# Expert inputs gathered by a token list per slot instead of scattered row by row, with routing and experts in one block

## The reference, cut to what matters

```python
logits = xt @ router_w
probs = jax.nn.softmax(logits, axis=-1)
top1 = jnp.argmax(probs, axis=-1)
...
top2 = jnp.argmax(logits_no1, axis=-1)
...
loc1 = jnp.cumsum(m1, axis=0) - 1.0
loc2 = jnp.cumsum(m2, axis=0) - 1.0 + m1.sum(axis=0, keepdims=True)
C = 2 * math.ceil(T / E)
m1 = m1 * (loc1 < C)
m2 = m2 * (loc2 < C)
...
xin = jnp.einsum('tec,td->ecd', dispatch, xt)
h = jnp.einsum('ecd,edf->ecf', xin, fc1_w) + fc1_b[:, None, :]
h = jax.nn.gelu(h, approximate=False)
eout = jnp.einsum('ecf,efd->ecd', h, fc2_w) + fc2_b[:, None, :]
...
moe_out = jnp.einsum('tec,ecd->td', combine, eout).reshape(b, s, D)
return resid + moe_out
```

## Time and profile before

| what | value |
|---|---|
| median of three runs | 2062.14 us |
| the three runs | 2052.34, 2062.14 and 2062.99 us |
| the profiled execution | 2056.92 us |
| its span in the profile | 2055.2 us |
| busy: PE, DVE, ACT, POOL | 1669.1, 1533.7, 1170.0, 847.3 us |

### The profile page before, as it was taken

The page is one execution under the profiler, slowest core; times in us unless marked ns, Lnnn a source line. Parts: engine busy times, 40 slices in busy tenths (PEclk is TensorE's granted clock), DMA queues, the critical chain, the costliest instruction groups (busy, mean ns, idle before and its releaser), DMA issues. The chain is left out here.

```text
span 2055.2 us, 42001 instructions
## 1 busy us (share of the span) xinstructions
PE 1669.1 (81%) x15556; PEld 804.9 (39%) x15556; DVE 1533.7 (75%) x2709; ACT 1170.0 (57%) x2150; POOL 847.3 (41%) x1066
## 2 busy tenths in 40 slices
PE   5799999997799999999999627799999995501992
PEld 2666666664133333333332224233333332400771
DVE  4767888877899999999999367788888883550124
ACT  3232222225499898898988614577777774300332
POOL 1100000005488878778788525122121122074454
PEclk8789999998699999999999857799999998555996
DMA  2186000004101011001110035111111114111444
GB/s 80 63 139 88 0 0 0 0 0 144 32 21 37 20 22 37 20 22 31 26 21 5 23 87 150 38 38 34 36 32 38 39 23 98 48 48 51 138 134 143
DMA packets 96025, 103.06 MB, mean 50 GB/s; under 512 B 28288, under 2 KB 62800, under 8 KB 95344
## 3 DMA queue, kind: packets, MB, share of 16 engines
q1 hardware_dynamic: 91760, 92.33, 19.2%
q0 software_dynamic: 4096, 8.43, 1.2%
HBM read 63.65 MB, written 36.80 MB: 49 GB/s over the span
## 5 line engine op out<-in xcount | busy, mean ns | idle before, releaser
L1234 DVE TENSOR_REDUCE ba_at_top<-ps 128x2 f32<-128x1024 f32 x512 | 588.4, 1217 | 18.0 <-PE ps L1149 16.2
L1267 ACT ACTIVATE ba_at_ring<-ps 128x512 f32<-128x512 f32 x1024 | 556.9, 597 | 64.8 <-PE ps L1175 51.4
L1313 POOL TENSOR_TENSOR ba_at_ring<-ba_at_ring,rb_near 128x256 f32<-128x256 f32 (+2 forms) x640 | 483.2, 783 | 148.2 <-ACT ba_at_ring L1267 142.3
L1234 DVE TENSOR_REDUCE ca_at_top<-ps 128x2 f32<-128x1024 f32 (+3 forms) x384 | 348.6, 954 | 68.6 <-PE ps L1149 33.0
L1267 ACT ACTIVATE ca_at_ring<-ps 128x512 f32<-128x512 f32 (+1 forms) x640 | 318.7, 553 | 98.7 <-PE ps L1175 96.6
L1175 PE MATMUL ps<-qop,kop 49*128 49x512 bf16 (+3 forms) x1792 | 321.6, 367 | 35.2 <-DMA qop<-ca_at_negm 7.2
L1149 PE MATMUL ps<-kop,qop 48*128 48x512 bf16 (+3 forms) x1792 | 316.7, 368 | 32.2 <-DVE ba_at_top L1234 12.4
L1194 PE MATMUL ps<-ba_at_ring,ba_at_low 128*32 128x256 f32 (+1 forms) x4864 | 329.6, 358 | 12.7 <-ACT ba_at_osb L1254 9.8
L1303 POOL TENSOR_SCALAR_AFFINE_SELECT ca_at_ring<-ca_at_ring 128x512 f32<-128x512 f32 x128 | 80.0, 637 | 359.3 <-ACT ca_at_ring L1267 359.2
L520 ACT ACTIVATE gm_sg<-ps,gm_bias 128x512 f32<-128x512 f32 x128 | 88.1, 688 | 235.0 <-PE ps L460 235.0
L1175 PEld LDWEIGHTS ps<-qop,kop 49*128 49x128 bf16 x1792 | 81.5, 93 | 351.2 <-ACT ba_at_ring L1267 189.0
(11 more groups left out here) (316 smaller groups left out, 1728.6 us busy)
## 6 DMA issues: line engine op xcount, KB each, us to landing
cs_fc<-in_fc_w SPq DMA_DIRECT2D x32, 256.0 KB, 2.7
qk_parts<-ba_at_ring SPq DMA_DIRECT2D x24, 256.0 KB, 3.7
qop<-qk_parts SPq DMA_DIRECT2D x64, 96.0 KB
kop<-qk_parts SPq DMA_DIRECT2D x64, 96.0 KB
qk_parts<-ca_at_ring SPq DMA_DIRECT2D x24, 256.0 KB, 3.6
ex_xi<-expert_rows_in SPq DMA_DIRECT2D x16, 258.0 KB, 3.1
expert_rows_in<-gm_zero SPq DMA_DIRECT2D x1, 4096.0 KB
expert_rows_out<-gm_zero SPq DMA_DIRECT2D x1, 4096.0 KB
```

The lines of the kernel that those rows point to most:

```text
L1234: nc.vector.tensor_reduce(top[:, k0 // CH, half, :, pair, i % HB], k.ps[:, slot:slot + 2, 0:k1 - k0], AX.X, ALU.max).then_inc(a_read, 1)
L1267: nc.scalar.activation(ring[:, ring_of(u, n) * HG + t % HG, 0:width(n)], k.ps[:, B_BANK + bank_of(u, t), 0:width(n)], ACT.Exp).then_inc(ex ...
L1313: ins = nc.gpsimd.tensor_tensor(w, w, a.near[:, u % NG * HG + j, lo - (i - 1) * P:hi - (i - 1) * P], ALU.mult)
```

## The change

The rows of the tokens are no longer sent to slots. SP writes the normalised tokens once, in token order, to `expert_rows_in` (four plain DMAs, now 4096 rows of 128 words). For each of the 8192 slots the kernel makes the number of the pair that sits in it, as a table `cs_rows` of 128 x 64 integers (slot = 128 times column plus partition), and POOL gathers the rows of an expert by four indirect DMAs that read, `ex_xi` from `expert_rows_in`. The same table, in its other half, tells where the results go.

The table is made with matmuls. For each choice DVE splits the slot number of each token into column and partition (a cast, a shift, an and, a cast back) and makes two one-hot arrays in bf16: `ids`, 128 x 32 x 64, which has a one at the slot's column, and `same`, 128 x 32 x 128, which has a one at its partition. They lie in the tiles `qop` and `kop` of the attention, which are free by then. ACT multiplies `ids` by the token's partition number, POOL by its tile number, and PE adds `same` transposed times these over the 32 tiles: 64 matmuls of 128 x 128 x 128 in all, into one bank. Seven small DVE instructions turn the sums into row numbers, with a row of its own for each unused slot.

`route` and `experts` become one block: `experts` now hands back five functions that each engine calls at the end of its part of `route`. `ex_xi` and `ex_eo` have four buffers instead of two, the loop over experts is written out, and POOL fetches three experts ahead. The addition of the gated hidden state to `x_tok` moves from the end of `route` into the loop over experts on DVE, a quarter after each of four experts. The zeroing of `expert_rows_in` in the first mixture, the copy of the tokens on ACT and the row-number column go away.

```diff
-                sp.dma_start(k.rows_in[0:E * CAP, 0:D].rearrange("(p a) d -> p a d", p=P),
-                             zero[:, 0:D].unsqueeze(1).broadcast_to([P, E * CAP // P, D])).then_inc(cleared, 16)
-                sp.dma_start(k.rows_in[0:E * CAP, D:D + 1].bitcast(I32).rearrange("(p a) b -> p (a b)", p=P), m["unused_rows"],
-                             allow_slow_non_contiguous=True).then_inc(cleared, 16)
...
+                for b in range(B):
+                    sp.wait_ge(dve_plain, (b + 1) * TB // 2)
+                    sp.wait_ge(act_plain, (b + 1) * TB // 2)
+                    sp.dma_start(k.rows_in[b * L:(b + 1) * L, :].rearrange("(t p) d -> p t d", p=P),
+                                 r.xt[:, b * TB:(b + 1) * TB, :]).then_inc(r.sent, 16)
+                then.sync(sp)
...
+                for i in range(2):
+                    pe.wait_ge(weighed, i + 1)
+                    pe.wait_ge(by_tile, i + 1)
+                    for t in range(NT):
+                        ins = nc.tensor.matmul(k.ps[:, 7, 0:2 * NSLOT], same[:, i, t, :],
+                                               ids[:, i, t, :, :].rearrange("p o c -> p (o c)"),
+                                               start=i == 0 and t == 0, stop=i == 1 and t == NT - 1)
+                ins.then_inc(tabled, 1)
+                then.tensor(pe)
...
-                for b in range(B):
-                    ts = slice(b * TB, (b + 1) * TB)
-                    nc.scalar.copy(r.xt[:, 1, ts, 0:D], r.xt[:, 0, ts, 0:D]).then_inc(copied, 1)
+                for i in range(2):
+                    act.wait_ge(alike, i + 1)
+                    nc.scalar.activation(ids[:, i, :, 1, :], ids[:, i, :, 0, :], ACT.Copy,
+                                         scale=rc[:, T_PART:T_PART + 1]).then_inc(weighed, 1)
...
-                send_copies(nc, k, r, 0)
-                pool.wait_ge(to_ready, 2)
-                pool.wait_ge(copied, B)
-                send_copies(nc, k, r, 1)
+                    pool.wait_ge(weighed, i + 1)
+                    tile = rc[:, T_TILE + i * NT:T_TILE + (i + 1) * NT].unsqueeze(2).broadcast_to([P, NT, NSLOT])
+                    nc.gpsimd.tensor_tensor(ids[:, i, :, 0, :], ids[:, i, :, 0, :], tile, ALU.mult).then_inc(by_tile, 1)
+                then.gpsimd(pool)
...
-                    vec.tensor_copy(r.to[:, i, :], row[:, i, :]).then_inc(to_ready, 1)
+                    L_(vec.tensor_copy(numi[:, 0, :], row[:, i, :]))
+                    L_(vec.tensor_scalar(numi[:, 1, :], numi[:, 0, :], 7, None, ALU.logical_shift_right))
+                    L_(vec.tensor_scalar(numi[:, 2, :], numi[:, 0, :], P - 1, None, ALU.bitwise_and))
+                    L_(vec.tensor_copy(numf[:], numi[:, 1:3, :]))
+                    vec.tensor_tensor(ids[:, i, :, 0, :], rc[:, T_IOTA:T_IOTA + NSLOT].unsqueeze(1).broadcast_to([P, NT, NSLOT]),
+                                      numf[:, 0, :].unsqueeze(2).broadcast_to([P, NT, NSLOT]), ALU.is_equal)
+                    vec.tensor_tensor(same[:, i, :, :], rc[:, T_IOTA:T_IOTA + P].unsqueeze(1).broadcast_to([P, NT, P]),
+                                      numf[:, 1, :].unsqueeze(2).broadcast_to([P, NT, P]), ALU.is_equal).then_inc(alike, 1)
...
+                dve.wait_ge(tabled, 1)
...
+                vec.tensor_scalar(r.rows[:, 1, :], r.rows[:, 0, :], TOK - 1, None, ALU.bitwise_and).then_inc(table_ready, 1)
+                then.vector(dve)
...
+    def gpsimd(pool):
+        def fetch(e):
...
+            if e >= XB:
+                pool.wait_ge(turned, e - XB + 1)
+            for q in range(QT):
+                at = e * QT + q
+                nc.gpsimd.indirect_dma_start(xi[:, e % XB, q, :], None, k.rows_in,
+                                             bass.IndirectOffsetOnAxis(ap=r.rows[:, 1, at:at + 1], axis=0)).then_inc(x_in[e % XB], 16)
...
+        def give(e):
+            pool.wait_ge(eo_ready, e + 1)
...
+        pool.wait_ge(r.table_ready, 1)
+        pool.wait_ge(r.sent, B * 16)
+        for e in range(XB - 1):
+            fetch(e)
+        for e in range(E):
+            if e + XB - 1 < E:
+                fetch(e + XB - 1)
+            give(e)
...
+        turn(0)
+        for e in range(E):
+            if e + 1 < E:
+                turn(e + 1)
+            upper(e)
+            if e:
+                lower(e - 1)
+        lower(E - 1)
```

More of the change, by code:

```diff
@@ L1572, in flat, with _ @@
             return t[:].rearrange("p t e -> p (t e)")
+        then = experts(nc, k, m, r, c)
         with nc.Block() as block:
-            block.sync(r.loads)
+            @block.sync
+            def _(sp):
+                r.loads(sp)
+                for b in range(B):
[4 more added lines that the diff above has]
+                then.sync(sp)
             @block.tensor
@@ new lines, in scalar @@
+    def scalar(act):
+        act.wait_ge(consts_in, 32)
+        for e in range(E):
+            for f in range(FB):
+                act.wait_ge(up, e * FB + f + 1)
+                if f == 0 and e >= 2:
+                    act.wait_ge(down, e - 1)
+                nc.scalar.activation(hh[:, e % 2, f, :], k.ps[:, 2 + f, :], ACT.Gelu, bias=b1[:, e, f:f + 1]).then_inc(act_done, 1)
+        act.wait_ge(r.g_ready, 1)
+        for t in range(NT):
+            n = t // 4
+            if t % 4 == 0:
+                act.wait_ge(got[n % 4], (n // 4 + 1) * 2 * 16)
+            y1 = back[:, 0, n % 4, t % 4, :]
+            nc.scalar.activation(y1, y1, ACT.Copy, scale=r.g[:, 0, t:t + 1]).then_inc(first, 1)
@@ new lines, in vector, with turned_in, out, residual @@
+    def vector(dve):
+        dve.wait_ge(consts_in, 32)
+        def turned_in(e):
+            dve.wait_ge(turned, e + 1)
+            if e >= 2:
+                dve.wait_ge(up, (e - 1) * FB)
+            nc.vector.tensor_scalar(xT[:, e % 2, :], k.ps[:, e % 2, :], r.ln2[:, 0:1], r.ln2[:, 1:2], ALU.mult, ALU.add).then_inc(xT_ready, 1)
+        def out(e):
+            dve.wait_ge(down, e + 1)
+            if e >= OB:
+                dve.wait_ge(eo_out[e % OB], QT * 16 * (e // OB))
+            row = b2[:, e:e + 1, :].broadcast_to([P, QT, D])
+            nc.vector.tensor_tensor(eo[:, e % OB, :, :], k.ps[:, 6 + e % 2, :].rearrange("p (q d) -> p q d", d=D), row, ALU.add).then_inc(eo_ready, 1)
+        def residual(b):
+            h = r.hidden[:, b * TB:(b + 1) * TB, :]
+            xs = k.x[:, b * TB:(b + 1) * TB, :]
+            nc.vector.tensor_tensor(h, h, k.row[:, 2, b:b + 1, :].broadcast_to([P, TB, D]), ALU.mult).then_inc(gated_h, 1)
+            dve.wait_ge(gated_h, b + 1)
+            nc.vector.tensor_tensor(xs, xs, h, ALU.add).then_inc(x_plain, 1)
+        def add(n):
+            xs = k.x[:, 4 * n:4 * n + 4, :]
+            dve.wait_ge(gated, n + 1)
+            dve.wait_ge(x_plain, B)
+            nc.vector.tensor_tensor(xs, xs, back[:, 1, n % 4, :, :], ALU.add).then_inc(summed, 1)
+        turned_in(0)
+        for e in range(E):
+            if e + 1 < E:
+                turned_in(e + 1)
+            if e:
+                out(e - 1)
+                if e % 3 == 0 and e // 3 <= B:
+                    residual(e // 3 - 1)
+        out(E - 1)
+        for t in range(NT):
+            dve.wait_ge(first, t + 1)
+            y1, y2 = back[:, 0, t // 4 % 4, t % 4, :], back[:, 1, t // 4 % 4, t % 4, :]
+            nc.vector.scalar_tensor_tensor(y2, y2, r.g[:, 1, t:t + 1], y1, ALU.mult, ALU.add).then_inc(both, 1)
+            if t % 4 == 3 and t >= 7:
+                add(t // 4 - 1)
+        add(NCH - 1)
@@ L2010, in causal_sublayer @@
         route(nc, k, m, r)
-        experts(nc, k, m, r)
 def program(nc, m):
```

329 lines of the change are left out of this document (112 added, 217 removed).

## The result

| | median | executions |
|---|---|---|
| before | 2058.93 us | 12 (2051.04 to 2063.84) |
| after | 2068.57 us | 12 (2060.73 to 2073.44) |

The ratio is 1.0049, with a 95% interval of 1.0036 to 1.0062: some 10 us slower, on the line between "no change" and "slower" that the prediction drew at 0.5%. The forecast was 2065.

The account below looks back on a forecast made before the run. POOL's issuing of 128 indirect DMAs behind the table was to bound the experts. At full clock -4.7 us, plus 10.7 for clock falls, made +6.0 on the profiled 2056.92, 2062.9, and 1.7 more gave 2065 us; range 2044 to 2086.

Parts of the forecast that it names:

- What bounds: Experts: POOL's issuing bounds, eight issues or 10.13 us an expert against PE's 7.45; 128 issues are 161.9 us.
- The table: Ahead of the experts: added DVE instructions +7.3 us; POOL's first fetch at 1841.7, 43.2 later than the old first send.
- A fetch's price: POOL's gathers: a fetch costs what a send costs, a pitch of 1.265 us; no indirect read in the trace before.
- rivals of a dearer and of a cheaper fetch: POOL's fetch pitch: 1.48, about 2078 us, chance 0.26; or 1.0 or less, about 2041 to 2046, chance 0.16.
- second rival: L1792 on POOL: fetch pitch 1.48, +19.8 us, about 2078; passes 0.5% from about 1.38 on; chance 0.26.
- fourth rival: POOL's issuing is hardly a cost, so PE bounds from about 1854: -41 us, about 2018; chance 0.04.
- The waits: POOL in the expert loop: start 5.7 us, middle none if PE's clock holds, end 6.5; residual pieces slow it 1.4.
- The clock: PE: 2.7 us pauses drop the clock every second expert, some six times, +10.7 us; earlier 1.6 us pause fell, 1.3 held.
- slack of 0.57: Middle experts: the chain from fetch end to dependent give, 9.56 us, stays under POOL's 10.13 us an expert.
- The rival in which the clock holds: PE during the experts: no clock falls, so -4.7 us, about 2054; chance 0.15.
- What was put at nothing: First mixture's zeroing, at most -2 us; SP's token writes, far ahead of 1841; SP's loads and ACT's copy, off the path.
- The sum: Whole kernel: -4.7 us at full clock, +10.7 for clock falls, together +6.0; forecast 2065 us.

Follow-up runs that it names:

- the run with two fills: Kernel after, four buffers, PE running two matmuls of constants before each turn from the fourth expert on: 2064.29 us, ratio 1.0035.

## Why the prediction was right, step by step

**What bounds.** Right: POOL's issuing takes over from the sequence of POOL and PE, at ten us an expert against 7.45. Six buffers and half the fetches showed it from two sides. As forecast, POOL's 162 us of issuing begin some 43 us later (44.7 measured) than the old 84.

**The table.** DVE's added instructions were put at +7.3 us on the second choice's slot; measured are 10.13 (67.46 less 57.33), of which 2.79 are the held-up instruction and 7.34 the added ones. That hold-up is the step that the prediction lacks. POOL's multiply was put at 4.7 and took 3.62, less than the bounds of 4.7 and 5.5, and the other pieces fit within 0.3; so the first fetch came only 1.5 us late, two misses of opposite sign.

**A fetch's price.** Right: the prediction took a send's price for a fetch, for which it had no row, and that came true. Measured is a pitch of 1.25 for fetches (0.947 and 0.30) and 1.27 for sends, where 1.265 was taken for both. Bare issuing of all 128 is 162.7 us (161.4 to the last start, and one slot), where the sum had 162.1 with the longer first issue. The rivals of a dearer and of a cheaper fetch both fall on this row. The pitch of 1.38 at which the second rival was to pass 0.5% does not come out of its own sum: from +6.0, 4 us over 64 fetches pass 10 us, a pitch of 1.33. The fourth rival falls too, as taking 32 fetches off POOL shortened the stretch by 29.7 us against six buffers. By the rule of the Trainium skill's page "DMA: Bandwidth & Descriptors", section "Issuing engines are not separate DMA queues", the move to POOL would be nearly free; these runs disagree.

**The waits.** Start 5.7 forecast, 6.1 measured; end 6.5 against 4.2; the residual's long issues 1.4 against 2.5 (four issues of 1.42 to 1.72 us in place of 0.95 to 0.97; with six buffers they cost 2.8).

**The clock.** Right in kind, to the number of falls: every second expert, six times in the middle, because POOL's wait lets the next expert's rows land. Wrong in size, and this is the largest mis-sized term: 10.7 forecast, 14.05 measured. A fall was priced at 2.36 from the first upper alone. The rows above show that the turn ahead of it runs slow too, 1.12 for 0.66 or 0.60, and the upper 6.01 to 6.10 for 3.60; that is 2.9 together, less the slack of 0.57 is 2.3, a little short of what five of the six waits show (2.49 to 2.70). Some of the rest is the slack: fetches landed 2.5 us after issue, where the chain of 9.56 us took 2.3 from the sends, so about 0.4 was left. The sixth wait, 1.11, stands behind the shortest slow upper, 4.62. The rival in which the clock holds falls with the same rows.

The falls decide the sign, as forecast: -4.7 was expected without them, and +10.8 less 14.05 is -3.3, an estimate that takes all six waits for theirs. But that the clock would fall was inferred from a premise that did not hold, and in that the prediction was lucky. The 1.6 and 1.3 us of the earlier trace rows are stretches inside pauses of 1.90 and 1.47 us, and in the run with 64-row fetches the clock held after pauses of 2.92 and 2.98 us (upper 3.60 behind both); the second of them, from the timeline:

```profile
1970.91 0.66 PE L1845 MATMUL ps<-cst,ex_xi 128*128 128x128 f32 x4 [2.98 <-DMA ex_xi<-expert_rows_in,cs_rows]
1971.40 3.60 PE L1854 MATMUL ps<-ex_xT,cs_fc 128*128 128x512 f32 x8
```

So a pause of 2.7 us at each expert need not have brought the clock down. The pauses ahead of the six falls were 4.0 to 5.8 us, one at every second expert.

**What was put at nothing.** The zeroing that went away, issued from 125.8 us on, gained nothing that shows. The first mixture's first product (PE's line, first and last start) before and after:

```profile
L459 PE MATMUL ps<-hT,gm_w x256: 592/595/1201, 105.3 to 456.0; 128*128 x112, 128*128 128x512 f32 x16
```
```profile
L455 PE MATMUL ps<-hT,gm_w x256: 592/595/1222, 105.0 to 456.9; 128*128 x112, 128*128 128x512 f32 x16
```

The stage runs 351 us with the transfers and 352 without. SP's four writes of the tokens were issued by 1780.2 and landed at most 7.5 us later, 60 us ahead of the first fetch.

**The sum.** +6.0 forecast, +10.8 in the stage: +1.5 for the table, +3.3 for the clock, +1.1 for the residual, -1.9 for the waits at the start and the end, and +0.8 in the issues. The total of 2065 came nearer to the measured 2068.6 than this, 3.6 us. It was set against 2058.6, the mean of four executions, which the median of twelve, 2058.9, bears out; the medians, which differ by 9.6 and not by 10.8, also hold what lies ahead of the block and behind the last send.

## What to carry to other kernels

When one engine issues all indirect DMAs, count them times the issue pitch first, whatever the transfers cost, and set that against the work of the engine that consumes them; then give the issuing engine enough buffers that it never waits for a result, because each of its waits is lost for good. An engine that feeds a faster one makes it pause, and the pause costs a second time where the consumer's clock falls, but only if the consumer's delay comes back to the feeder: with two more buffers the clock still fell, and POOL did not wait. Work of POOL that reads the on-chip memory belongs where DVE is idle.

## What the runs showed of the hardware that was not expected

- An indirect DMA of 128 rows costs POOL 0.94 us and one of 64 rows 0.90: nearly all of that time is the instruction's.
- A POOL multiply of 3.62 us stretched a DVE instruction of 0.18 us on a single input to 3.59, and one on two inputs from 0.69 to 3.48; begun beside a DVE instruction of two inputs it took 5.70 itself.
- The granted clock fell after pauses of 1.91 and 2.37 us and held after one of 2.58 in the run with two fills, and held after one of 2.98 in the run with 64-row fetches; PE had worked at full clock ahead of each. The length of the last pause alone, by which the prediction went, does not decide it. What else does was not settled by these runs.
